# Decoder layer with attention, state-space scan and experts on one core: an earlier copy of transposed probabilities, a later copy of logits, more unread matmuls

## What is computed

```
x = ln(x + attention(x))                  # causal, 16 heads of 16
x = ln(x + ssm(ctx, z=x))                 # in-projection, 4-tap convolution, silu, then per channel e
    state = state * exp(delta_t * A) + (delta_t * u_t) * B_t     # 256 channels x 16 states, 256 time steps
    y_t = sum_n(state * C_t);  y = (y + D * u) * silu(z)
x = ln(x + experts(x))                    # router: softmax, best 2 of 8
    h = silu(0.5 * x @ w_gate[e]) * (x @ w_up[e]) @ w_down[e] * 0.25
```

## Time and profile before

| | |
|---|---|
| median of 3 runs | 411.48 us (410.95 to 412.12) |
| profiled execution | 411.99 us, its span 410.2 us |
| TensorE busy | 342.3 us (83%), mean granted clock 0.955 |
| VectorE busy | 255.3 us (62%) |
| GpSimd busy | 236.3 us (58%) |
| ScalarE busy | 208.8 us (51%) |

### The profile page before, as it was taken

How to read it: one execution, slowest core, us unless ns; L and a number is a source line. 1 busy time by engine, 2 the same in 40 slices (tenths; PEclk the granted TensorE clock), 3 DMA queues, 4 the chain that set the end, 5 groups by cost and what they waited for, 6 DMA issues and landing times.

```text
span 410.2 us, 5831 instructions
## 1 busy us (share of the span) xinstructions
PE 342.3 (83%) x1860; PEld 202.5 (49%) x1860; DVE 255.3 (62%) x442; ACT 208.8 (51%) x488; POOL 236.3 (58%) x223
## 2 busy tenths in 40 slices
PE   7796678778777687887778878999999999999971
PEld 3363335534346344653435433566666666666541
DVE  2999989897998989689898872222222222222234
ACT  4689798687857788849773112212232222222103
POOL 3076888999999968977789214122332233322214
PEclk9999699987989989998998998999999999999996
DMA  7060111430111210293008941011111111111063
GB/s 215 10 109 20 34 53 38 173 99 27 43 62 51 77 54 27 77 303 110 27 26 287 377 157 51 14 38 53 51 39 40 51 53 40 43 47 38 27 218 102
DMA packets 29455, 34.47 MB, mean 84 GB/s; under 512 B 4074, under 2 KB 23826, under 8 KB 29426
## 3 DMA queue, kind: packets, MB, share of 16 engines
q1 hardware_dynamic: 24770, 26.36, 20.3%
q0 software_dynamic: 2208, 6.03, 4.9%
q10 hardware_dynamic: 2448, 1.71, 1.4%
HBM read 28.92 MB, written 5.18 MB: 83 GB/s over the span
## 4 chain that ended last, share of the span: by engine, by line
PE 36%; DVE 5%; ACT 3%; DMA 2%; POOL 2%; issue 2%; DVEq 0%; POOLq 0%; ACTq 0%
PE psS L1649 19%; PE psD L1668 5%; PE psO L1668 5%; PE psD L1659 2%; PE psT L1644 1%; DMA c_rows<-z_out 1%; POOL rstd L500 1%; ACT experts L692 1%; DMA delta<-x_rows,row_in 1%; PE psS L1460 1%; DMA z_out<-delta,row_out 1%; DVE experts L986 1%; DVE u_sb L1160 1%; PE psT L1488 1%; PE psT L1411 0%
## 5 line engine op out<-in xcount | busy, mean ns | idle before, releaser
L1649 PE MATMUL psS<-experts,delta 128*128 x184 | 86.5, 593 | 0.5 <-ACT delta L820 0.5
L511 POOL TENSOR_TENSOR experts<-experts,c_rows 128x1024 f32<-128x1024 f32 x31 | 73.4, 2369 | 17.3 <-DVE experts L986 17.0
L986 DVE TENSOR_TENSOR_SCAN experts<-experts,psD 128x512 f32<-128x512 f32 x64 | 74.3, 1202 | 0.1
L575 POOL DMA_INDIRECT z_out<-delta,row_out x23 | 22.7, 988 | 88.5 <-ACT delta L834 88.5
L1237 DVE COPY u_sb<-psD 128x512 f32<-128x512 f32 x23 | 15.9, 691 | 68.7 <-PE psD L1659 68.7
L692 ACT ACTIVATE experts<-delta,A_sb 128x255 f32<-128x255 f32 x128 | 54.7, 518 | 0.0
L1411 PE MATMUL psT<-ident,probs_at 128*128 128x128 f32 x192 | 32.0, 291 | 24.2 <-ACT probT L730 24.2
L1649 PEld LDWEIGHTS psS<-experts,delta 128*128 128x128 f32 x184 | 33.1, 190 | 24.3 <-issue 23.3
L974 DVE TENSOR_TENSOR psD<-du,psD 128x512 f32<-128x512 f32 x64 | 41.0, 685 | 2.2 <-PE psD L1369 2.2
L1245 DVE TENSOR_TENSOR du<-du,psS 128x512 f32<-128x512 f32 x23 | 15.8, 687 | 37.3 <-PE psS L1649 37.3
L1411 PEld LDWEIGHTS psT<-ident,probs_at 128*128 128x128 f32 x192 | 22.0, 146 | 33.9 <-ACT probT L730 33.2
(11 more groups left out here) (243 smaller groups left out, 588.0 us busy)
## 6 DMA issues: line engine op xcount, KB each, us to landing
c_rows<-c_dram SPq DMA_DIRECT2D x32, 256.0 KB, 3.3
experts<-in_L_ffn_w_gate_dram SPq DMA_DIRECT2D x8, 512.0 KB, 7.1
experts<-in_L_ffn_w_up_dram SPq DMA_DIRECT2D x8, 512.0 KB, 8.1
experts<-in_L_ffn_w_down_dram SPq DMA_DIRECT2D x8, 512.0 KB, 8.8
x_in<-in_x_dram SPq DMA_DIRECT2D x4, 256.0 KB, 4.7
x_rows<-x_sb SPq DMA_DIRECT2D x4, 256.0 KB, 2.2
probs_at<-z_out SPq DMA_DIRECT2D x4, 256.0 KB, 4.8
c_rows<-z_out ACTq DMA_DIRECT2D x4, 256.0 KB, 5.4
```

What stands on the lines that cost most here:

```text
L511: pool.tensor_tensor(states[:, g % ST], states[:, g % ST], c_rows[:, g % CR].rearrange("p n (o s) -> p n o s", o=1).broadcast_to([P, 2, HA ...
L986: dve.tensor_tensor_scan(states[:, g % ST, n].rearrange("p h s -> p (h s)"), dA[:, g % DA, n].rearrange("p h s -> p (h s)"), psD[:, n, :], ...
L1649: ins = pe.matmul(psS[:, bank, :], xgT[:, s % 2, k, :], gate_up_of(bass.ds(e, 1), i)[:, k, :], start=(k == 0), stop=(k == FC - 1))
```

## The change

There are three edits. ScalarE: in the second step of each batch (m = 1) it copies the first transposed group of the batch's first attention group ahead of the step's decay factors, instead of after them. VectorE: the copy of the logits moves from the end of the seventh step (m = 6) into the eighth, between its multiplications and its scan. TensorE: in the first step of the program 17 instead of 14 unread matmuls, in the second step 4 new ones, and in both steps 3 new ones between the two broadcasts, all into `psT`.

```diff
@@ ScalarE
                 for m in range(NP):
                     g = NP * b + m
+                    if m == 1:
+                        take_probT(GROUPS * b, 0)
                     if 0 < g < STEPS - 2:
                         if (g + 2) % NP == 0:
                             act.wait_ge(du_rdy, (g + 2) // NP + 1)
                         decay(g + 2)
                     G = GROUPS * b + m
                     for r in range(GH):
-                        if 1 <= m <= 4 and r < 3:
+                        if 1 <= m <= 4 and r < 3 and (m, r) != (1, 0):
                             take_probT(G - 1, r)
@@ VectorE
                     multiply_b(g)
+                    if m == 7 and f >= 0:
+                        take_logits(f)
                     if g == 0:
                         maxima(0)
...
                     if m == 1 and f >= 0:
                         gate_sum(f)
-                    elif m == 6:
-                        if f >= 0:
-                            take_logits(f)
                     elif m == 7:
@@ TensorE
                     if g == 0:
-                        keep_warm(14, psT[:])
+                        keep_warm(17, psT[:])
+                    elif g == 1:
+                        keep_warm(4, psT[:])
                     if m < GROUPS:
                         broadcast_b(g + 1, 0)
+                        if g < 2:
+                            keep_warm(3, psT[:])
                         broadcast_b(g + 1, 1)
```

## The result

| | before | changed |
|---|---|---|
| median | 411.8 us (8 runs, 410.95 to 412.71) | 416.98 us (8 runs, 413.24 to 419.72) |
| profiled execution, span | 411.99, 410.2 us | 417.1, 415.3 us |
| mean granted clock in it | 0.955 | 0.952 |

The ratio is 1.0095, 95% interval 1.0062 to 1.0127: the change makes the kernel slower by about 1% (2.6 to 5.2 us). Runs more than 1.5% above the fastest of their kernel (here the one of 419.72, in the experiments up to 855.1) count in the medians but not in the ratios and mean clocks. The eight times scatter more widely than the eight before, but that is not the change's doing: beside the experiments the kernel before scatters from 410.45 to 417.8 us.

What follows compares the result with a forecast made beforehand. VectorE's work plus its waits was taken to bound the state-space steps. +1.0 (early copy) + 0 + 0 - 0.55 (logits) = +0.45 us, giving 412.45, or 411.9 moved to the median; range 410.0 to 413.9.

Steps and rivals of the forecast that it cites:

- Part 1, the counted waits: Second step, batches 1 to 3: early copy adds 0.67 us wait, saves 0.22 and 0.03, delays last exponentials about 0.43.
- Part 1, what the clock does with them: Third steps, batches 1 to 3: a tenth of each shift comes back through TensorE's clock; total +1.0 us, bounds +0.6, +1.5.
- The sign that the prediction gave: Third steps of batches 1 to 3: VectorE's waits for scores of 2.1 to 2.9 us would show it right.
- Rival A: Early copy leaves TensorE some 2.0 us idle between second and third groups, lowering its clock; 413.6 us, chance 0.2.
- Batch 0: Second step of batch 0: ScalarE's third copy comes 0.4 to 0.9 us earlier, hidden by the scan; gain 0.
- Part 2: Unread matmuls in the first two steps: cost 0 at full clock, clock gain in batch 0 hidden; 0, down to -0.3.
- Part 3: Logits copied behind the eighth step's multiplications: +0.2, -0.67, -0.07 in batches 1 to 3; sum -0.55, bounds -0.9 and +0.3.
- the +0.2 forecast: Batch 1, moved logits: later transposes delay the broadcast ahead of the output projection by 0.2 to 0.35 us; +0.2 taken.
- the -0.67 forecast: Batch 2, moved logits: output projection starts at 174.35 instead of 175.02, and VectorE gets all of it.
- the forecast -0.1: Batch 3, moved logits: VectorE's gain turns into a wait for the output projection; at most -0.1 us.
- its cover: Batch 3: room for the moved `multiply_last` to slow beside GpSimd's addition, bounded by one whole addition more, about 1.2 us.
- Its chance of 0.18 for a faster kernel: Whole kernel: chance of under 410.25 us, from the clock holding (0.13) and half of the early copy not waiting (0.07).

Runs made afterwards that it cites:

- experiment 1: Kernel before with only ScalarE's early copy of the first group, in all batches: 417.88 us against 412.64, ratio 1.0119.
- experiment 9: Kernel before with the early copy in all batches, plus five unread matmuls ahead of the second group in batches 1 to 3: 415.13 us against 413.18, ratio 1.0049.
- Experiment 3: Kernel before with only the changed kernel's additional unread matmuls: 413.03 us, ratio 1.0003.
- experiment 2: Kernel before with only the copy of the logits moved into the eighth step: 414.04 us, ratio 1.0014.
- experiment 4: Changed kernel without its additional unread matmuls, so both moved copies against the kernel before: 416.46 us, ratio 1.0061.
- experiment 8: Kernel before with the first copy between the decay factors' halves and the logits moved in batch 2 alone: 413.64 us, ratio 1.0011.
- experiment 11: Kernel before with the logits copied in the eighth step in batch 3 alone: 414.31 us, ratio 1.0013.
- experiment 6: Kernel before with the early copy in batch 0 alone: 413.31 us, ratio 1.0010.
- experiment 10: Kernel before with the first copy between the decay factors' halves and two unread matmuls before the second group: 413.21 us, ratio 1.0008.
- experiment 5: Kernel before with the first copy between the two halves of the decay factors in every second step: 412.23 us, ratio 1.0006.
- experiment 7: Kernel before, old order, with one unread 0.40 us activation behind the second step's decay factors in batches 1 to 3: 416.64 us, ratio 1.0101.

## Why the prediction was wrong

**Part 1, the counted waits: right.** New wait (0.58 instead of 0.67), old waits, the 0.64 from transposes to copy and the gap of 2.0 us are there; 1.50 and 1.51 against 1.04 at full clock say +0.46, where +0.43 was counted.

**Part 1, what the clock does with them: wrong, and this is the step that failed.** The prediction took the low clock in the third step as given, because the one profile of before had it in all three batches, and asked only how +0.43 adds to waits of 1.72 and 2.41; it even let a part come back, and so came to +1.0 (+0.6 to +1.5). Most runs of the kernel before are not like that profile. Their mean clock is 0.964, and the four profiles with ScalarE's order unchanged in batches 1 to 3 show waits of 1.03 to 1.05 in batches 1 and 3. With the gap at 2 us the fall becomes usual: nine of eleven third steps, against four of twelve with a gap near the old one. (The sign that the prediction gave, waits of 2.1 to 2.9 us there, held in one batch of three.) Such a fall shows as 0.5 to 1.4 us on top of 1.5 in the wait for scores, and there are further losses behind it. Measured, the term is not +1.0 but +4.9 us (experiment 1, 3.3 to 6.6), of which 2.9 go when the gap is filled (experiment 9). The profile before hid this, because its total was typical all the same: its batches 1 to 3 took 148.4 us, 2 us more than 146.2 to 146.5, and its preparation 34.0 us where most profiles show 36. What decides whether the clock falls in a given run, at the same gap, stays open.

**Rival A named the mechanism**, with its place (the gap of some 2.0 us behind the second group) and its sign (the third group at 1.11 us), but priced it from the same profile: 0.69 for two batches, since batch 1 was thought to be low already, and gave it 0.2. 413.6 stood where 417.0 was measured. Its argument against, that a later low stretch ends within the same work, did not hold: in most runs the stretch was absent before, not late.

**Batch 0: right.** 41.82 and 41.84 us; the gain is hidden by the scan.

**Part 2: right.** Experiment 3 is within 0.4 us by its median and 0.1 by its ratio, and its interval holds zero; the second step's broadcasts are in time in the changed kernel too.

**Part 3: the waits right, the total not seen.** Batch 1: the wait before the residual grew from 1.18 to 1.36 us in the changed kernel (1.39 in experiments 2 and 4), the +0.2 forecast. Batch 2: -0.56 by experiment 8 against the -0.67 forecast. Batch 3: VectorE's gain turned into a wait for the projection (1.56 us), as forecast, and where the clock was full (experiment 11) the batch is 0.13 us shorter than in experiment 6, the forecast -0.1. `multiply_last` moved beside GpSimd's addition and took 1.94 us instead of 1.23, inside its cover. By the Trainium skill's page "SBUF — State Buffer", section "Who interferes with whom", an instruction of this kind and GpSimd's reads exclude each other, so it would have begun only after the addition that ends at 225.90, and with its 1.23 ended at 227.1. It ends at 226.98, so the trace agrees to 0.15 us. What the term left out is again the clock: with all three logits moved its mean was 0.950 against 0.964. Where that comes from stays open. In the changed kernel the output projection of batch 3 ran wholly at the lower level (from the logits' copy to the residual 5.97 us against 4.99), which would fit, but experiment 11 did not settle it. The kernel of experiment 2, too, shows no loss in batches 1 to 3 of its profile (146.5 us, as experiment 3).

**The range** ended at 413.9, because every bound in it was taken from rows of one execution. (Its chance of 0.18 for a faster kernel is 0.165 by its own two parts; nothing hangs on that.) In the same sense the profile after shows 5.1 us of which 2.3 lie in a stage that the change does not touch.

## What to carry to other kernels

Where TensorE waits in short bursts for another engine's copies, a delay of 0.4 us can cost more than 0.4 us: it can tip the clock, and here that made 4 to 5 us out of a counted 1.4. Before a copy is moved ahead of other work, ask whether its input is ready; the same copy two activations later cost nothing that could be measured. And take the clock's part from many runs: one profile's clock (0.955) may not be that of the kernel (0.964), and neither its low stretches nor their absence are a base for a sum.

## What was not expected of the hardware

The clock fell with no gap between TensorE's groups longer than 2.04 us in the stretch before (9 of 11 cases at 1.97 to 2.04), and a gap of 1.57 was survived in 8 of 11. Five unread matmuls (1.25 us of work) in the gap of experiment 9 kept it at full level in all three batches of its profile, while the kernel lost 0.49% instead of 1.19%.

The same instructions of the preparation take 34.0 us to the first scan in one execution and 36.4 in another, by one low stretch at 20 us. And VectorE's four step-size instructions take between 5.8 us (experiment 3) and 7.6 (before): the shortest of them 0.67 us, the longest 2.74, beside a product of GpSimd of 2.81 us. What is won there can be lost again one batch later. In experiments 3, 6, 8, 10 and 11 these instructions took 5.8 to 5.9 us; TensorE then waited 2.42 to 2.44 us for GpSimd's product (line 511) in the first step of batch 2, the clock fell behind that wait, and VectorE waited 3.6 us for the scores of the second step. In the kernel before and experiments 4, 5, 7 and 9 the instructions took 6.4 to 7.6 us, TensorE waited 0.3 us or less there, and VectorE 0.5.
